# A ternary weight matrix from one sign pass and one compare-and-minimum, in place of two sign passes and an addition

## The reference

```python
def ternary_quant(W):
    scale = jnp.mean(jnp.abs(W))
    q = jnp.clip(jnp.round(W / (scale + 1e-08)), -1.0, 1.0) * scale
    return W + jax.lax.stop_gradient(q - W)

z = x_flat @ ternary_quant(W_syn).T + b_syn        # 512 -> 2048
topv, _ = jax.lax.top_k(z, k)                      # k = 204 of 2048
hidden = jnp.where(z >= topv[:, -1:], jax.nn.relu(z), 0.0)
out = hidden @ ternary_quant(W_out).T + b_out      # 2048 -> 512
return layernorm(x + out, gamma, beta)
```

## Time and profile before

| | |
|---|---|
| time, median of 3 runs | 966.49 us (965.68 to 966.95) |
| profiled execution, from its first to its last instruction | 964.9 us |
| TensorE busy | 920.8 us, 95% |
| VectorE busy | 846.3 us, 88% |
| GpSimd busy | 755.3 us, 78% |
| ScalarE busy | 586.6 us, 61% |
| chain that ended last | TensorE 89%, VectorE 6% |

### The profile page before, as it was taken

One profiled execution on the slowest core, in us unless ns is written; L12 is line 12 of the kernel. 1 busy time (PEld: TensorE's weight loads), 2 busy tenths in 40 slices (PEclk: granted clock), 3 DMA queues, 4 the chain that ended last, 5 costly groups with the idle time before them and its releaser, 6 DMA issues.

```text
span 964.9 us, 19094 instructions
## 1 busy us (share of the span) xinstructions
PE 920.8 (95%) x6823; PEld 488.0 (51%) x6823; DVE 846.3 (88%) x2290; ACT 586.6 (61%) x778; POOL 755.3 (78%) x655
## 2 busy tenths in 40 slices
PE   5848999999999999999999999999999999999986
PEld 2424655555555555554555555455555545555544
DVE  6879989988888998888899888888988888898897
ACT  6789646666555566655556666555666655566562
POOL 1546888887888888888888888988888898888863
PEclk9978999999999999999999999999999999999999
DMA  9887854664654466466547546544564664456532
GB/s 333 259 202 121 143 86 86 114 112 97 120 101 97 86 112 114 96 120 107 98 85 108 119 90 121 113 98 87 99 121 93 116 118 101 85 93 121 99 77 55
DMA packets 322371, 111.08 MB, mean 115 GB/s; under 512 B 308448, under 2 KB 308704, under 8 KB 321504
## 3 DMA queue, kind: packets, MB, share of 16 engines
q1 hardware_dynamic: 318432, 102.42, 54.9%
q10 hardware_dynamic: 3840, 7.41, 2.1%
HBM read 24.34 MB, written 8.39 MB: 34 GB/s over the span
## 4 chain that ended last, share of the span: by engine, by line
PE 89%; DVE 6%; SPq 1%; DMA 1%; issue 1%; ACT 0%; ACTq 0%; POOL 0%; DVEq 0%; POOLq 0%
PE proj L969 47%; PE p_ffn L1104 10%; PE p_ffn L1074 10%; PE p_wo L1118 8%; PE p_av L1039 3%; PE sbank L1030 3%; PE p_av L1050 3%; PE sbank L977 1%; DMA area<-in_L_attn_Wk_dram 1%; PE sbank L1165 1%; SPq L280 1%; DVE cand L1489 1%; SPq L275 1%; PE p_ffn L1090 1%; DVE area L1589 0%
## 5 line engine op out<-in xcount | busy, mean ns | idle before, releaser
L969 PE MATMUL proj<-wqkv,xT 128*128 128x512 f16 x1152 | 261.6, 385 | 0.0
L969 PE MATMUL proj<-wsynT,xT 128*128 128x512 f16 x1024 | 240.3, 383 | 4.6 <-DMA wsynT<-xrn 2.4
L969 PEld LDWEIGHTS proj<-wqkv,xT 128*128 128x128 f16 x1152 | 112.5, 99 | 127.8 <-issue 6.0
L969 PEld LDWEIGHTS proj<-wsynT,xT 128*128 128x128 f16 x1024 | 95.5, 98 | 107.3 <-issue 6.1
L761 POOL TENSOR_TENSOR hl<-area,hl 128x2048 f16<-128x2048 f32 x31 | 128.5, 4145 | 4.1 <-ACT hl L561 4.1
L473 ACT ACTIVATE area<-area 128x1024 f16<-128x1024 f32 x64 | 64.1, 1049 | 104.2 <-POOL area L719 104.2
L1074 PE MATMUL p_ffn<-woutT,area 128*128 128x512 f16 x480 | 109.3, 378 | 0.0
L1489 DVE MAX8 cand<-area 128x8 f32<-128x128 f32 x512 | 107.8, 278 | 1.1
L1104 PE MATMUL p_ffn<-woutT,area 128*128 128x512 f16 x480 | 108.6, 379 | 0.0
L1379 DVE SCALAR_TENSOR_TENSOR area<-proj,c,gb 128x512 f32<-128x512 f32 x128 | 92.2, 741 | 5.3 <-PE proj L969 5.3
L766 POOL TENSOR_TENSOR ahl<-pair_a,ahl 128x512 f16<-128x512 f32 x32 | 37.1, 1158 | 74.9 <-DVE area L1589 70.0
(11 more groups left out here) (253 smaller groups left out, 1818.3 us busy)
## 6 DMA issues: line engine op xcount, KB each, us to landing
xrn<-in_L_attn_x_dram SPq DMA_DIRECT2D x32, 256.0 KB, 3.3
out_dram<-pair_b SPq DMA_DIRECT2D x29, 256.0 KB, 2.0
woutT<-in_L_ffn_W_syn_dram ACTq DMA_DIRECT2D x2, 1024.0 KB, 10.9
area<-in_L_ffn_W_syn_dram ACTq DMA_DIRECT2D x2, 1024.0 KB, 11.9
woutT<-in_L_ffn_W_out_dram SPq DMA_DIRECT2D x2, 1024.0 KB, 7.1
area<-in_L_attn_Wq_dram ACTq DMA_DIRECT2D x1, 1024.0 KB, 7.0
area<-in_L_attn_Wk_dram ACTq DMA_DIRECT2D x1, 1024.0 KB, 9.5
area<-in_L_attn_Wv_dram ACTq DMA_DIRECT2D x1, 1024.0 KB, 11.6
```

Source lines behind the costliest of these rows:

```text
L969: last = nc.tensor.matmul(bank, xT[:, b.par, k, :], w, start=m == 0, stop=m == len(pairs) - 1)
```

## The change

For each quarter, one sign pass is left, sign(0.99999994 W + thr), which is 1 or -1. VectorE then computes min(W > thr, sign), where the comparison gives 1 or 0: the result is -1, 0 or 1. The scale `so` loses its factor 0.5. Since VectorE now reads the raw weights after the sign pass, the waits that guarded them against overwriting (`out_sign`) become waits for VectorE's instruction (`out_tern`). Waits that guarded `signs_b`, `ahl` and `xhl` are dropped.

```diff
             def out_transpose(q):
-                sp.wait_ge(S[f"out_tern{q}"], 2 if q == 3 else 1)
+                sp.wait_ge(S[f"out_tern{q}"], 1)
             def high_transposed(u):
                 if u.n == 0:
-                    sp.wait_ge(S["out_sign"], 9)
+                    sp.wait_ge(S["out_tern1"], 1)
             def step(sp, i, p):
                 if b and b.n == 1:
-                    sp.wait_ge(S["out_sign"], 5)
+                    sp.wait_ge(S["out_tern3"], 1)
                     out_transpose(2)
                     out_transpose(3)
             def attention_high(u):
-                if u.n == 0:
-                    act.wait_ge(S["out_tern3"], 2)
             def normalised(a):
-                if a.n == 3:
-                    act.wait_ge(S["out_tern3"], 2)
             def hidden_high(u, src):
                 if u.n == 0:
-                    act.wait_ge(S["out_sign"], 7)
+                    act.wait_ge(S["out_tern0"], 1)
             def first_step():
-                sign("out", out_in[2], signs_b, out_thr[1])
                 sign("out", out_in[2], out_t[2], out_thr[0])
-                sign("out", out_in[3][:, 0:N // 2], halves_3[0], out_thr[1])
-                wait(act, "xT_ready", Tile(1, 0), 16, 16)
-                sign("out", out_in[3][:, N // 2:N], halves_3[1], out_thr[1])
                 sign("out", out_in[3], out_t[3], out_thr[0])
                 attention_out(t)
                 qk_high(Tile(0, 1))
-                act.wait_ge(S["out_tern2"], 1)
-                sign("out", out_in[0], signs_b, out_thr[1])
                 act.wait_ge(S["outT2"], 16)
                 sign("out", out_in[0], out_t[0], out_thr[0])
             def second_step():
-                act.wait_ge(S["out_tern0"], 1)
-                sign("out", out_in[1], signs_b, out_thr[1])
                 act.wait_ge(S["outT0"], 16)
                 sign("out", out_in[1], out_t[1], out_thr[0])
             def ternary_of_signs(q, n):
                 dve.wait_ge(S["out_sign"], n)
-                if q < 3:
-                    nc.vector.tensor_tensor(out_t[q], out_t[q], signs_b, ALU.add).then_inc(S[f"out_tern{q}"], 1)
-                else:
-                    for l in range(2):
-                        part = out_t[q][:, l * N // 2:(l + 1) * N // 2]
-                        nc.vector.tensor_tensor(part, part, halves_3[l], ALU.add).then_inc(S["out_tern3"], 1)
+                nc.vector.scalar_tensor_tensor(out_t[q], out_in[q], out_thr[0], out_t[q], ALU.is_gt,
+                                               ALU.min).then_inc(S[f"out_tern{q}"], 1)
             def network_out(d):
-                if d.n == 0:
-                    dve.wait_ge(S["out_tern1"], 1)
             def initial_step():
-                ternary_of_signs(2, 2)
+                ternary_of_signs(2, 1)
-                ternary_of_signs(3, 5)
+                ternary_of_signs(3, 2)
             def following_step():
-                ternary_of_signs(0, 7)
+                ternary_of_signs(0, 3)
-                then(nc.vector.scalar_tensor_tensor(so, scale_out, 0.5 * XS / 16384.0, pc[:, 43:44], ALU.mult,
+                then(nc.vector.scalar_tensor_tensor(so, scale_out, XS / 16384.0, pc[:, 43:44], ALU.mult,
-                ternary_of_signs(1, 9)
+                ternary_of_signs(1, 4)
```

More of the change, by code:

```diff
@@ L163, in build @@
         out_t = [slot4, slot4, slot4, slot3]
-        halves_3 = [ahl.rearrange("p a g c -> p (a g c)"), xhl.rearrange("p a n -> p (a n)")]
         proj = [pb("proj0"), pb("proj1")]
```

## The result

The changed kernel takes 970.88 us (median of 5 runs, 969.58 to 971.76), the kernel before 966.49: a ratio of 1.0046 with a 95% interval of 1.0034 to 1.0058, or 4.4 us (3.3 to 5.6) slower. Timed again, among the experiments, it was 1.0043 (1.0030 to 1.0056).

A forecast was written before the change was run, and what follows sets the result against it. TensorE bounds 27 of 31 steps and keeps any delay from the first two, which VectorE sets. VectorE's 2.4 us plus 2.1 from the hidden-layer transposes' gate made 4.5, 969.4 on the profiled span, 971.0 timed; range 968.8 to 974.5.

The forecast's parts named there:

- ScalarE's relief: First two steps: removing four quarters' sign passes, some 8 us of ScalarE, counted as nothing because VectorE is waited for.
- the half rate (F): VectorE's four new instructions run at half rate, 4.6 us each; delay grows to +13.7, 980 us; chance 0.03.
- the additions' rate (D): VectorE's new instruction is no slower than the additions, 1.13 us; about -0.2 to 0, 966.3 us; chance 0.03.
- I take 0 for both together: VectorE, first two steps: GpSimd's disturbance, +0 to +0.4 per quarter, against up to 0.6 regained at L1609; range -0.6 to +1.6.
- the sum had 2.4: Step 1: VectorE's longer work makes TensorE's wait at 98.21 end 2.4 us later.
- the gate on the hidden layer's transposes: Gate (c), SyncE: tile 0's `high_transposed` waits for quarter 1's instruction, 107.0 instead of 100.2; 2.1 us beyond VectorE's delay.
- the second wait that the sum had in its middle: First network product's low half: low part lands at 115.1 after 6.1 us, so this half begins 4.5 us late.
- the third gate: Gate (c): SyncE's `high_transposed` of tile 0 waits for quarter 1's instruction, going at 107.0 instead of 100.2, +6.9 us.
- the first and third together: Gate (a), SyncE's transposes of quarters 2 and 3 held from 76.7 to 79.2; gate (c), `high_transposed` moved +6.9 us.
- The near tie (b): ScalarE's `hidden_high` waits for quarter 0's ternary, +3.4 us, delaying GpSimd's `attention_low`; counted as nothing, 0.7 with full 6.08.
- C, the clock: TensorE's new gaps before and within the first network product bring half speed, 973.0 to 975.5 us; chance 0.14.
- B: Landings are quicker and VectorE gains at L1609, so only VectorE's delay stays: 968.3 to 969.8 us; chance 0.16.

The follow-up runs named there:

- gates-with-short-operation run: Changed kernel with its gates, VectorE's instruction replaced by a two-input f16 minimum without the compare: 967.09 us, ratio 1.0004 to the kernel before.
- The gates alone: Kernel before, sign passes and addition kept, with only the three waits moved behind VectorE's additions: 967.57 us, ratio 1.0002.
- opening the third: Changed kernel, quarter 1's compare reading the bias row, `high_transposed` waiting for its sign pass; run twice: 970.69 and 971.43 us, ratios 1.0054 and 1.0045 to the kernel before.
- with the other two gates open: Changed kernel, compare on the bias row, first and third gates back on the signs, `hidden_high` still waiting for quarter 0's instruction: 969.51 us, ratio 1.0048 to the kernel before.
- two experiments: Changed kernel, compare on the bias row, all gates back on the signs: 974.64 us; kernel before, `high_transposed` also waiting for tile 1's selection flag: 974.58 us.
- the run with the third gate further off: Kernel before with one added wait: `high_transposed` of tile 0 also waits for the selection's flag of tile 1; 974.58 us, ratio 1.0084.

## Why the prediction was right

It said 971.0 us, and 970.88 was measured. That the two agree to 0.1 us is luck: one term was too small by some 1.3 us, and another, of 2.1, was mostly not there.

*Right.* VectorE sets the two steps and the full stretch keeps the delay: shown by the two uniform windows and by the gates-with-short-operation run, in which four shorter instructions bring the time back. ScalarE's relief is worth nothing: shown. The undisturbed row of the new instruction, 2.35 us from L1432, was 2.34 for quarter 0. Neither the half rate (F) nor the additions' rate (D) occurred. Of the wait positions, quarter 2's transpose near 79.3 against 78.23 and `hidden_high` near 94.3 against 93.50 were right for a prologue 2.1 us shorter only within about 1.3 us, and the hidden layer's first transpose near 107 against 106.58 within 1.7, all on the late side.

*Mis-sized: "I take 0 for both together"*, the term for GpSimd's disturbance less L1609's gain. The instructions took 4.6 us more and not 2.99, and 0.6 came back: +1.0 net. The price of up to 0.4 for a quarter came from one row, L1541; what sets it is how much of GpSimd's row is left when VectorE's begins, 1.08 us for quarter 2. The prediction put the 2.16 us of the old addition down to L697, but that began at 74.14, a us behind it; by the reckoning above it was the row ahead, with 1.08 us left (1.08 + 1.22 = 2.30, 0.14 too long again):

```profile
72.91 1.27 POOL L696 TENSOR_TENSOR xrn<-xrn,boutx 128x512 f32<-128x512 f32 x1
```

With the waits that followed in step 1 (0.56 for the first count, 0.29 before L1465) the fourth scores were 3.7 us late, where the sum had 2.4.

*Failed: the 2.1 us of "the gate on the hidden layer's transposes"*, as a cost on top. TensorE did wait for the high part, 1.76 us, but the second wait that the sum had in its middle did not come: 6.1 us of landing was taken from one row and was 5.0 in the changed kernel. In the trace the network product was in fact 5.6 us late, 1.9 more than the fourth scores, near the 2.1. But VectorE was late by then as well, so with the gate open part of TensorE's time went into a wait for VectorE's flag and a longer next step. The gates alone measured +0.2 (-0.7 to +1.1), and opening the third gave nothing that the timed runs can tell. Most of the slowdown is the instruction's, not half of it. The traces leave 0.4 us for the third gate and 0.8 for the first and third together; whether it is some tenths or one us stays open.

*The near tie (b)* was one: VectorE's third product of the scores began at 101.75, at once behind GpSimd's `attention_low`, which ended at 101.66. What the prediction missed there was the sign: with the other two gates open, this gate made the kernel faster, +4.6 instead of +7.2 us. The changed kernel without this gate alone was not run.

*Rivals.* C, the clock, did not occur in the changed kernel (its clock is 1.00 from 87 us on), but did with a gap of 5.4 us in two experiments. In step 0 the clock's pattern did shift: the 12 matmuls behind the transposes of q took 3.83 us instead of 4.67, but in step 1 TensorE waited for other engines all the same (0.41, 0.98 and 1.40 us), so nothing came of it. B had the mechanism's proportions (mostly VectorE), with a price that was too small.

## What to carry to other kernels

Count the engine that the stage waits for, not the instructions: here 8 us of ScalarE's work was exchanged for 4.6 us of VectorE's, and only the second was on the path. An f16 addition replaced by an operation that reads f32 cost twice as much for the same width here (2.34 against 1.22 us), and more yet where GpSimd was at work on two inputs as well (2.60 to 3.23). And a wait that looks like a pure cost may keep two engines in a good order; look at who begins first before opening it.

## What the runs showed of the hardware

- VectorE's two-input instructions and GpSimd's hold each other up, and it matters which begins first: L1589 ahead of GpSimd's L761 by 0.2 us took 2.35 while L761 took 6.08, against 4.1 in the mean of its 31; begun 1.3 us behind it, the same product took 5.24 us and GpSimd 4.36. The Trainium skill (SBUF — State Buffer, section "Who interferes with whom") says that the two share a pair of ports as an exclusive lock and that the order of issue, not the shape, decides which of them blocks. The traces agree, if the one behind stands still until the first has ended: 95.04 - 92.91 + 4.1 = 6.2 against 6.08 for GpSimd, and 98.76 - 95.67 + 2.35 = 5.4 against 5.24 for VectorE. Where several short rows follow each other the two take turns, and rows on both sides grow: quarter 2's instruction waited for L683 and L684 for it (3.23 and 3.32 us, 3.43 and 3.46 by the same sum).
- For short instructions it is worse in proportion, since what they wait for is the rest of the other's row: the 128 x 32 selection product took 0.25, 0.85 or 1.26 us, and GpSimd's 128 x 128 addition L764 2.38 instead of 0.46 beside quarter 3's instruction.
- In the changed kernel TensorE's gaps of 0.98, 1.40 and 1.76 us between 95 and 111 us left the granted clock at 1.00; in the run with the third gate further off one of 5.38 us brought it to 0.50, and the matmuls behind it were still at 0.50 between 113 and 114 us.
